# A shifted-window transformer block: unit 0's first norm ahead of the pipeline's steps, and 32x32 block transposes of neighbouring tokens

## The chip, the cores and the metric

The kernel runs on one core of one Trainium2 chip. The metric is the device time of one execution in microseconds. Five engines work from queues of their own, each in program order: TensorE (PE, with its weight loads as PEld), VectorE (DVE), ScalarE (ACT), GpSimd (POOL) and SyncE (SP), which here issues nearly all DMAs.

## The reference

`x` is [16, 192, 56, 56] in fp32 (batch, channels, height, width). Cut to what matters:

```python
xl = transpose(x, (0, 2, 3, 1))                       # channels last
xl = (xl - mean) * rsqrt(var + 1e-5) * n1w + n1b      # first norm, over the 192 channels
xl = roll(xl, (-3, -3), axis=(1, 2))                  # shifted windows of 7x7 tokens
q, k, v = split(xw @ qkv_w.T + qkv_b)                 # 6 heads of 32
attn = softmax(q @ k.T * 32 ** -0.5)                  # within each window, no mask
out = (attn @ v) @ proj_w.T + proj_b
xl = roll(windows back to the image, (3, 3))
xl = layernorm(xl, n2w, n2b)                          # second norm
h = gelu(xl @ fc1_w.T + fc1_b) @ fc2_w.T + fc2_b      # 192 -> 768 -> 192
return transpose(h, (0, 3, 1, 2)) + x
```

The first norm's mean and variance belong to a token (one pixel), over its 192 channels, while the input and all activations lie with channels in partitions.

## The kernel before, in words

**Units.** The work is cut into 128 units (`UNITS`): one row of eight 7x7 windows of one image, T = 392 tokens. A unit passes through a software pipeline. Each engine's program is written out by hand as a `step(t, k, it)` function in which `u[lag]` is the unit `t - lag`, or None where that is outside 0 to 127, and `steps` (L470) emits the steps t = 0 to 134. The order of the calls within a step is the order of the engine's queue. TensorE works on QKV of unit t, attention of t - 1, projection of t - 2 and the MLP of t - 3 (L621). VectorE's numbering begins earlier, with the transposes: QKV of unit u on TensorE needs what VectorE does in its step u + 2.

**First norm.** SP loads each unit twice. `load_groups` (L382) puts it into `xg`, of which partition 32r + c holds channel c of each group of 32 for the tokens 128r to 128r + 127; `load` (L374) puts it into `xt` with channels in partitions. `token_blocks` (L948) is one VectorE instruction that transposes `xg` in blocks of 32x32 into `xtok`, tokens in partitions; block b of the four (`PAIRS`) takes every fourth token, so partition p then holds tokens 4p to 4p + 3. `stats(0, u, j)` and `mean_var(0, u, j)` (L966, L975) reduce the channels to mean and variance in `mv[0]`, four tokens a partition. GpSimd's `rstd` (L1185) makes 1/sqrt(var + eps) with a power. `stats_out` (L391) stores `mv[0]` to a little DRAM tensor in the order of the tokens, 32 bytes a partition, in one DMA, and `stats_in` (L398) broadcasts it to all partitions (`bc`, 392 KB). Then `less_mean` and `times_rstd` (L955, L962; channels 0 to 127, VectorE) and `less_mean_rest` and `times_rstd_rest` (L1194, L1201; channels 128 to 191, GpSimd) normalise. ScalarE's `hi_part` (L718) rounds that to the high part `x1_h` (and `x_r`), and VectorE's `lo_part` (L1000) subtracts for the low part. TensorE's `values` and `qkv` wait for `lo_part("x1", u, 1)`.

**Weights.** All weights are split into high and low parts on VectorE: those of QKV in `first_weights` (L911), which `less_mean(0)` calls and which also waits for TensorE's products of the bias (L505); all others, with the biases, in `other_weights` (L928), which `lo_part("x1", 0, 1)` calls. `other_weights` begins with a wait for ten small loads (`s_rest`), which SP issues at L424 to L432, behind `stats_out(0)`, `stats_in(0)`, `load_groups(2)` and `load(0, 1)`. The projection on TensorE waits for its end.

**SP's queue.** After the start (L413 to L432) each step (L447) is: `load_groups(t)`; for t below 7 also `load`; `stats_in(t - 2)`; the second half of `spread(t - 4)` and the first of `spread(t - 3)`, which copy V into the block-diagonal tile `vbd` once VectorE's `v_out` (L1061) has evicted it from PSUM; `stats_out(t - 1)`; then `store` (L405), which waits for GpSimd's `residual`, and the `load` that it makes room for.

**GpSimd's queue** (L1222) takes in one step, among others, `rstd(0, u[0])`, `less_mean_rest(u[1])`, `times_rstd_rest(u[1])` and then `rstd(1, u[4])`, the second norm's, on which VectorE's `normalise` (L983) waits.

Of the kernel before, what the change touches and what calls it, by code (L numbers as in the profile page):

```python
# [24 lines left out]
ALU = mybir.AluOpType  # L25
# [9 lines left out]
T = NW * N  # L35
# [6 lines left out]
PAIRS = NW // 2  # L42
# [57 lines left out]
def swin_block_program(nc, x, n1w, n1b, qkv_wt, qkv_b, proj_wt, proj_b, n2w, n2b,  # L100
                       fc1_wt, fc1_b, fc2_wt, fc2_b, out):
    ctx = ExitStack()
    with ctx:
        def sb(name, shape, dt=F32):
            return ctx.enter_context(nc.sbuf_tensor(name, shape, dt))
# [29 lines left out]


        xt = sb("xt", [128, SLOTS, 2, T])
        st = [sb(f"st{i}", [TP, PAIRS, 6]) for i in range(2)]
        mv = [sb(f"mv{i}", [TP, PAIRS, 2]) for i in range(2)]
        ve = [sb(f"ve{i}", [TP, PAIRS]) for i in range(2)]  # L140
        rs = sb("rs", [TP, PAIRS])


# [229 lines left out]
        def _(sp):  # L373
# [17 lines left out]
            def stats_out(u):  # L391
                sp.wait_ge(s_rs[0], nth(u, 1, 0))
                if u > 1:

                    sp.wait_ge(s_mr[u % 2], 16 * (u // 2))
                sp.dma_start(spread_out[u % 2].rearrange("(p b) q -> p b q", b=PAIRS), mv[0][:, :, :]).then_inc(s_mr_out, 16)

            def stats_in(u):  # L398
                sp.wait_ge(s_mr_out, 16 * (u + 1))
                if u > 1:  # L400
                    sp.wait_ge(s_ym1, nth(u - 2, 1, 0))
                    sp.wait_ge(s_yr1, nth(u - 2, 1, 0))
                sp.dma_start(bc[:, u % 2], spread_out[u % 2:u % 2 + 1].to_broadcast([128, T, 2])).then_inc(s_mr[u % 2], 16)
# [66 lines left out]
        def steps(step):  # L470

            for t in range(UNITS + LAGS):
                step(t, t % SLOTS, t // SLOTS)
# [405 lines left out]
        def _(dve):  # L879
# [68 lines left out]
            def token_blocks(u):  # L948
                dve.wait_ge(s_xg[u % XG], 16 * sum(len(group_runs(v % UPB)) for v in range(u % XG, u + 1, XG)))
                if u == 0:  # L950
                    dve.wait_ge(s_xg_zero, 1)
                nc.vector.transpose(xtok.rearrange("p b (c d) -> p c b d", d=32),
                                    xg[:, u % XG].rearrange("p c (t b) -> p c b t", b=PAIRS)).then_inc(s_tr, 1)

            def less_mean(u, k):  # L955
                if u == 0:
                    assert first_weights() == 4
                dve.wait_ge(s_mr[u % 2], 16 * (u // 2 + 1))
                dve.wait_ge(s_x[k], (u // SLOTS + 1) * transfers(k))
                nc.vector.tensor_tensor(ym1[:, :], xt[:, k, 0, :], bc[:, u % 2, :, 0], ALU.subtract).then_inc(s_ym1_sub, 1)  # L960

            def times_rstd(u):  # L962
                dve.wait_ge(s_ym1_sub, nth(u, 1, 0))
                nc.vector.tensor_tensor(ym1[:, :], ym1[:, :], bc[:, u % 2, :, 1], ALU.mult).then_inc(s_ym1, 1)

            def stats(ln, u, j):  # L966
                if ln == 0:
                    dve.wait_ge(s_tr, nth(u, 1, 0))
                    nc.vector.bn_stats(st[0][:, j, :], xtok[0:TP, j, :]).then_inc(s_stats[0], 1)
                    return  # L970
                if j % 2 == 0:
                    dve.wait_ge(s_pe["ln2"], nth(u, 2, j // 2))
                nc.vector.bn_stats(st[1][:, j, :], ln_chunk("ln2", j)).then_inc(s_stats[1], 1)

            def mean_var(ln, u, j):  # L975
                if j == 0:
                    dve.wait_ge(s_stats[ln], nth(u, PAIRS, PAIRS - 1))
                    if ln == 0 and u > 0:

                        dve.wait_ge(s_mr_out, 16 * u)  # L980
                nc.vector.bn_aggr(mv[ln][:, j, :], st[ln][:, j, :]).then_inc(s_mv[ln], 1)  # L981

            def normalise(ln, u, j):  # L983
# [16 lines left out]
            def lo_part(name, u, g):  # L1000
                xh, xl, xrr = HI_LO[name]
                lo, m, hi = ((xl, CM, xh), (xrr[CR:128], CR, xrr[0:CR]))[g]
                if name == "o":
                    dve.wait_ge(s_hi[name], nth(u, 5, 0))
                elif name == "x2":
                    dve.wait_ge(s_hi[name], nth(u, 3, 0))
                else:
                    dve.wait_ge(s_hi[name], nth(u, 2, g))
                src = evicted(name, g, m)
                if name == "o":  # L1010

                    nc.vector.scalar_tensor_tensor(out=lo, in0=src, scalar=bq[0:m, g:g + 1], in1=hi.bitcast(F32),
                                                   op0=ALU.add, op1=ALU.subtract).then_inc(s_lo[name], 1)
                else:
                    nc.vector.tensor_tensor(lo, src, hi.bitcast(F32), ALU.subtract).then_inc(s_lo[name], 1)
                if name == "x1" and g == 1 and u == 0:
                    other_weights(4)

            def hidden_lo(u, m):

# [47 lines left out]
            def step(t, k, it):  # L1068
# [2 lines left out]
                    less_max(u[4], 2)  # L1071
                    row_sum(u[4], 0)
                if u[1] is not None:
                    mean_var(0, u[1], 0)
                if u[4] is not None:
                    row_max(u[4], 3)
                    row_sum(u[4], 1)
                    row_scale(u[4], 0)
                if u[1] is not None:
                    mean_var(0, u[1], 1)  # L1080
                if u[6] is not None:
                    x2_rest_lo(u[6])
                if u[1] is not None:
                    mean_var(0, u[1], 2)
                if u[4] is not None:
                    less_max(u[4], 3)
                if u[5] is not None:
# [1 line left out]
                if u[7] is not None:  # L1089
                    finish_main(u[7], (k - 7) % SLOTS)  # L1090
                if u[1] is not None:
                    mean_var(0, u[1], 3)
                if u[3] is not None:
                    v_out(u[3], 0)
                if u[5] is not None:
# [1 line left out]
                if u[3] is not None:  # L1097
                    v_out(u[3], 1)
                if u[0] is not None:
                    token_blocks(u[0])  # L1100
                if u[5] is not None:
                    stats(1, u[5], 0)
                if u[0] is not None:
                    stats(0, u[0], 0)
                if u[7] is not None:
                    finish_rest(u[7])
                if u[5] is not None:
# [3 lines left out]
                if u[5] is not None:  # L1111
                    stats(1, u[5], 2)
                if u[2] is not None:
                    less_mean(u[2], (k - 2) % SLOTS)
                if u[6] is not None:
                    hidden_lo(u[6], 0)
                if u[5] is not None:
# [9 lines left out]
                if u[5] is not None:  # L1127
                    mean_var(1, u[5], 3)
                if u[2] is not None:
                    times_rstd(u[2])  # L1130
                if u[6] is not None:
                    hidden_lo(u[6], 1)
                    hidden_lo(u[6], 2)
                if u[0] is not None:
                    stats(0, u[0], 1)
                if u[4] is not None:
                    row_sum(u[4], 3)
                if u[5] is not None:
                    normalise(1, u[5], 0)
                    normalise(1, u[5], 1)  # L1140
                if u[0] is not None:
                    stats(0, u[0], 2)
                if u[5] is not None:
                    normalise(1, u[5], 2)
                    normalise(1, u[5], 3)
                if u[4] is not None:
                    row_scale(u[4], 3)
                if u[2] is not None:
                    lo_part("x1", u[2], 0)
                if u[3] is not None:  # L1150
                    row_max(u[3], 0)
                if u[6] is not None:
# [8 lines left out]
                if u[6] is not None:  # L1161
                    hidden_lo(u[6], 4)
                if u[2] is not None:
                    lo_part("x1", u[2], 1)
                if u[3] is not None:
                    row_max(u[3], 2)
                if u[0] is not None:
                    stats(0, u[0], 3)

            steps(step)  # L1170


        @block.gpsimd
        def _(pool):
# [10 lines left out]
            def rstd(ln, u):  # L1185

                pool.wait_ge(s_mv[ln], nth(u, PAIRS, PAIRS - 1))
                nc.gpsimd.tensor_tensor(ve[ln][:, :], mv[ln][:, :, 1], eps[0:TP, :], ALU.add).then_inc(s_ve[ln], 1)  # L1188
                pool.wait_ge(s_ve[ln], nth(u, 1, 0) + (2 if ln == 0 else 0))

                to = rs[:, :] if ln else mv[0][:, :, 1]
                nc.gpsimd.tensor_tensor(to, ve[ln][:, :], half[0:TP, 0:PAIRS], ALU.pow).then_inc(s_rs[ln], 1)

            def less_mean_rest(u, k):  # L1194
                pool.wait_ge(s_mr[u % 2], 16 * (u // 2 + 1))
                pool.wait_ge(s_x[k], (u // SLOTS + 1) * transfers(k))
                if u > 0:
                    pool.wait_ge(s_lo["x1"], nth(u - 1, 2, 1))
                nc.gpsimd.tensor_tensor(yr1[:, :], xt[0:CR, k, 1, :], bc[0:CR, u % 2, :, 0], ALU.subtract).then_inc(s_yr1_sub, 1)
# [22 lines left out]
            def step(t, k, it):  # L1222
                u = units(t)
                if u[4] is not None:
                    scaled_probs(u[4], 3)
                if u[6] is not None:
                    hidden_lo_last(u[6])
                if u[3] is not None:
                    scaled_probs(u[3], 0)
                if u[0] is not None:  # L1230
                    rstd(0, u[0])
                if u[1] is not None:
                    less_mean_rest(u[1], (k - 1) % SLOTS)
                    times_rstd_rest(u[1])
                if u[4] is not None:
                    rstd(1, u[4])
                if u[3] is not None:
                    scaled_probs(u[3], 1)
                if u[6] is not None:
                    residual(u[6], (k - 6) % SLOTS)  # L1240
                if u[3] is not None:
                    scaled_probs(u[3], 2)

            steps(step)


# [23 lines left out]
```

## Time and profile before

| | us |
|---|---|
| median of 3 runs | 2939.3 (2938.61 to 2942.02) |
| profiled execution, its own time | 2939.99 |
| its span | 2938.2 |
| PE, PEld busy in the span | 2888.9 (98%), 2820.7 (96%) |
| DVE, ACT busy | 2692.8 (92%), 2689.2 (92%) |
| POOL busy | 1365.5 (46%) |
| DMA, mean share of the 16 engines, q1 | 30.9% |

The span runs from the first to the last instruction of the profiled execution; its own time is 1.8 us more. Matmuls are pipelined, so that a busy PE is not PE at its peak. The granted TensorE clock has a mean of 0.999 of full speed. In the lists of waits a wait is put down to what came last by semaphore.

### The profile page before, as it was taken

What the parts mean: (1) busy time and instruction counts of PE and PEld (TensorE: products, weight loads), DVE (VectorE), ACT (ScalarE), POOL (GpSimd) and SP (SyncE); (2) the same over time, 40 slices, a digit from 0 to 9 for tenths busy, and PEclk for the clock granted to TensorE, in tenths of its full rate; (3) what the DMA queues carried; (4) which work ended last, traced back from release to release, by engine and by line L of the source; (5) the groups of instructions that cost most, each with busy time, mean ns of one, the idle gap of its engine ahead of it and who ended that gap; (6) DMA issues with size and microseconds to landing.
All of it is one profiled execution on the core that took longest, in us unless ns stands there. A gap on an engine that the chain in (4) does not pass through costs nothing.

```text
span 2938.2 us, 75046 instructions
## 1 busy us (share of the span) xinstructions
PE 2888.9 (98%) x26284; PEld 2820.7 (96%) x26284; DVE 2692.8 (92%) x7211; ACT 2689.2 (92%) x5500; POOL 1365.5 (46%) x1549
## 2 busy tenths in 40 slices
PE   4999999999999999999999999999999999999998
PEld 4999999999999999999999999999999999999998
DVE  7899999999999999999999999999999999999985
ACT  3899999999999999999999999999999999999996
POOL 3444444444444444444544444444445444444442
PEclk9999999999999999999999999999999999999999
DMA  5233333333333332333233233333333333333321
GB/s 111 61 76 75 70 75 75 74 68 78 77 70 71 74 78 68 75 78 70 71 74 78 69 73 79 70 69 77 78 70 71 76 76 69 75 75 73 69 60 26
DMA packets 606164, 213.11 MB, mean 73 GB/s; under 512 B 461411, under 2 KB 589156, under 8 KB 605796
## 3 DMA queue, kind: packets, MB, share of 16 engines
q1 hardware_dynamic: 601860, 206.64, 30.9%
q8 instruction: 217, 3.56, 0.5%
q10 hardware_dynamic: 3936, 1.68, 0.3%
q14 instruction: 151, 1.24, 0.1%
HBM read 130.69 MB, written 38.94 MB: 58 GB/s over the span
## 4 chain that ended last, share of the span: by engine, by line
PE 97%; DVE 1%; ACT 1%; SPq 0%; DMA 0%; issue 0%; POOL 0%; POOLq 0%; ACTq 0%
PE psum L318 8%; PE psum L319 7%; PE psum L320 7%; PE psum L322 7%; PE psum L321 7%; PE psum L600 7%; PE psum L574 6%; PE psum L554 5%; PE psum L565 5%; PE psum L555 5%; PE psum L566 5%; PE psum L556 5%; PE psum L580 4%; PE psum L328 4%; PE psum L330 3%; PE psum L329 3%
## 5 line engine op out<-in xcount | busy, mean ns | idle before, releaser
L1215 POOL TENSOR_TENSOR pr<-pr,rc 98x294 f32<-98x294 f32 x512 | 385.9, 764 | 382.3 <-DVE rc L1059 382.3
L756 ACT ACTIVATE hh<-psum,b 128x392 fp32r<-128x392 f32 x768 | 451.7, 588 | 46.2 <-PE psum L566 37.5
L759 ACT ACTIVATE hf<-psum,b 128x392 f32<-128x392 f32 x768 | 451.7, 588 | 6.3
L1188 POOL TENSOR_TENSOR ve<-mv,eps 98x4 f32<-98x4 f32 x256 | 80.9, 316 | 768.1 <-DVE mv L981 768.1
L1209 POOL TENSOR_TENSOR hl<-hf,hh 128x392 fp32r<-128x392 f32 x128 | 226.0, 1766 | 374.3 <-ACT hf L759 374.3
L1046 DVE TENSOR_REDUCE mx<-psum 98x6 f32<-98x294 f32 x512 | 232.3, 454 | 133.0 <-PE psum L575 129.0
L1023 DVE TENSOR_TENSOR hl<-hf,hh 128x392 fp32r<-128x392 f32 x640 | 347.7, 559 | 3.8 <-ACT hf L759 3.7
L318 PE MATMUL psum<-x_h,w_mh 128*128 128x392 f32 x768 | 275.0, 358 | 0.7 <-DVE pr L1051 0.6
L554 PE MATMUL psum<-hh,w2h 128*128 128x392 f32 x768 | 272.8, 355 | 0.0
L713 ACT ACTIVATE pt<-psum 113x294 f32<-113x294 f32 x512 | 207.1, 405 | 70.4 <-PE psum L580 70.2
L574 PE MATMUL psum<-km,qm 128*98 128x98 f32 x2048 | 261.0, 249 | 7.4 <-ACT qm L716 4.0
L565 PE MATMUL psum<-hl,w2h 128*128 128x392 f32 x768 | 264.5, 344 | 0.3 <-POOL hl L1209 0.3
L555 PE MATMUL psum<-hh,w2l 128*128 128x392 f32 x768 | 261.8, 341 | 0.0
L319 PE MATMUL psum<-x_h,w_ml 128*128 128x392 f32 x768 | 261.4, 340 | 0.0
L320 PE MATMUL psum<-x_l,w_mh 128*128 128x392 f32 x768 | 260.9, 340 | 0.0
L566 PE MATMUL psum<-hl,w2h 128*64 128x392 f32 x768 | 260.4, 339 | 0.0
L322 PE MATMUL psum<-x_r,w_rl 128*128 128x392 f32 x768 | 260.4, 339 | 0.0
L321 PE MATMUL psum<-x_r,w_rh 128*128 128x392 f32 x768 | 260.3, 339 | 0.0
L556 PE MATMUL psum<-hh,w2r 128*128 128x392 f32 x768 | 259.4, 338 | 0.0
L574 PEld LDWEIGHTS psum<-km,qm 128*98 128x98 f32 x2048 | 237.0, 166 | 11.3 <-ACT qm L716 4.6
L1051 DVE TENSOR_TENSOR pr<-psum,mx 98x294 f32<-98x294 f32 x512 | 234.2, 457 | 4.2
L768 ACT ACTIVATE pr<-pr 98x294 f32<-98x294 f32 x512 | 230.2, 450 | 7.7 <-DVE pr L1051 3.1
(144 smaller groups left out, 10410.3 us busy)
## 6 DMA issues: line engine op xcount, KB each, us to landing
bc<-mean_rstd SPq DMA_DIRECT2D x128, 392.0 KB, 3.7
vbd<-vs SPq DMA_DIRECT2D x1024, 36.8 KB
xg<-in_x SPq DMA_DIRECT2D x368, 96.0 KB, 2.4
xt<-in_x SPq DMA_DIRECT2D x112, 194.5 KB, 2.7
out<-xt SPq DMA_DIRECT2D x112, 194.5 KB, 1.9
xt<-in_x SPq DMA_DIRECT2D x112, 97.2 KB, 2.4
out<-xt SPq DMA_DIRECT2D x112, 97.2 KB, 2.1
xg<-in_x SPq DMA_DIRECT2D x128, 3.8 KB, 2.0
```

The costliest lines, as they stand in the source:

```text
L318: nc.tensor.matmul(ps, wmh[:, c0:c0 + m], xh, start=True, stop=False)
L319: nc.tensor.matmul(ps, wml[:, c0:c0 + m], xh, start=False, stop=False)
L320: nc.tensor.matmul(ps, wmh[:, c0:c0 + m], xl, start=False, stop=False)
L321: nc.tensor.matmul(ps, wrh[:, c0:c0 + m], xrr, start=False, stop=False)
L322: return nc.tensor.matmul(ps, wrl[:, c0:c0 + m], xrr, start=False, stop=True)
L554: nc.tensor.matmul(ym, w2h[:, m, 0:CM], hh[:, b, :], start=a, stop=False)
L555: nc.tensor.matmul(ym, w2l[:, m, :], hh[:, b, :], start=False, stop=False)
L565: nc.tensor.matmul(ym, w2h[:, m, 0:CM], hl[:, b, :], start=False, stop=z)
L566: nc.tensor.matmul(yx[0:CR], w2h[:, m, CM:C], hl[:, b, :], start=False, stop=z, skip_group_check=True).then_inc(s_pe["fc2"], 1)
L574: nc.tensor.matmul(ps[:, TP * wi:TP * wi + TP], qm[:, w, :], km[:, w, :], start=True, stop=True)
L756: nc.scalar.activation(hh[:, m % HB, :], bank("fc1", m)[:, 0:T], ACT.Gelu, bias=b1[:, m:m + 1]).then_inc(s_hh, 1)
L759: nc.scalar.activation(hf[:, m % HB, :], bank("fc1", m)[:, 0:T], ACT.Gelu, bias=b1[:, m:m + 1]).then_inc(s_gelu, 1)
```

## The change

It has three parts. (1) Unit 0's whole first norm (`token_blocks`, `stats`, `mean_var`, `less_mean` with `first_weights`, `times_rstd`, `lo_part`) stands on VectorE ahead of `steps`; behind it come unit 1's transpose, statistics and `mean_var`, then `other_weights(4)`. On GpSimd `rstd(0, 0)` and the two operations for channels 128 to 191 of unit 0 stand ahead of its steps. The calls for these units are left out of the steps by conditions; the other engines' order is not touched. Unit 2's statistics, which step 2 had around `less_mean(0)`, stay in step 2, now behind `other_weights`. (2) Block b of a transpose takes 32 neighbouring tokens: the source is contiguous where it had a stride of four floats, and partition 32r + t holds tokens 128r + 32b + t for b = 0 to 3. The 104 partitions that then hold tokens (`LP[0]`) take the place of 98. (3) `stats_out` becomes four DMAs with pieces of 8 bytes, 128 in each of three and 8 in the last, and the waits on `s_mr_out` count four times as much.

```diff
+        LP = (96 + T % 128, TP)
+        st = [sb(f"st{i}", [LP[i], PAIRS, 6]) for i in range(2)]
...
-                sp.dma_start(spread_out[u % 2].rearrange("(p b) q -> p b q", b=PAIRS), mv[0][:, :, :]).then_inc(s_mr_out, 16)
+                for r in range(3):
+                    sp.dma_start(spread_out[u % 2, 128 * r:128 * r + 128].rearrange("(b t) q -> t b q", b=PAIRS), mv[0][32 * r:32 * r + 32]).then_inc(s_mr_out, 16)
+                sp.dma_start(spread_out[u % 2, 384:T], mv[0][96:LP[0], 0, :]).then_inc(s_mr_out, 16)
...
             def stats_in(u):
-                sp.wait_ge(s_mr_out, 16 * (u + 1))
+                sp.wait_ge(s_mr_out, 16 * 4 * (u + 1))
...
                 nc.vector.transpose(xtok.rearrange("p b (c d) -> p c b d", d=32),
-                                    xg[:, u % XG].rearrange("p c (t b) -> p c b t", b=PAIRS)).then_inc(s_tr, 1)
+                                    xg[:, u % XG].rearrange("p c (b t) -> p c b t", b=PAIRS)).then_inc(s_tr, 1)
...
-                    nc.vector.bn_stats(st[0][:, j, :], xtok[0:TP, j, :]).then_inc(s_stats[0], 1)
+                    nc.vector.bn_stats(st[0][:, j, :], xtok[0:LP[0], j, :]).then_inc(s_stats[0], 1)
...
-                        dve.wait_ge(s_mr_out, 16 * u)
+                        dve.wait_ge(s_mr_out, 16 * 4 * u)
...
-                if name == "x1" and g == 1 and u == 0:
-                    other_weights(4)
...
                 if u[1] is not None:
-                    mean_var(0, u[1], 0)
+                    if u[1] > 1:
+                        mean_var(0, u[1], 0)
...
                 if u[0] is not None:
-                    token_blocks(u[0])
+                    if u[0] > 1:
+                        token_blocks(u[0])
...
                 if u[2] is not None:
-                    less_mean(u[2], (k - 2) % SLOTS)
+                    if u[2] > 0:
+                        less_mean(u[2], (k - 2) % SLOTS)
...
+            token_blocks(0)
+            for j in range(PAIRS):
+                stats(0, 0, j)
+            for j in range(PAIRS):
+                mean_var(0, 0, j)
+            less_mean(0, 0)
+            times_rstd(0)
+            lo_part("x1", 0, 0)
+            lo_part("x1", 0, 1)
+
+            token_blocks(1)
+            for j in range(PAIRS):
+                stats(0, 1, j)
+            for j in range(PAIRS):
+                mean_var(0, 1, j)
+            other_weights(4)
             steps(step)
...
                 if u[0] is not None:
-                    rstd(0, u[0])
-                if u[1] is not None:
-                    less_mean_rest(u[1], (k - 1) % SLOTS)
-                    times_rstd_rest(u[1])
+                    if u[0] > 0:
+                        rstd(0, u[0])
+                if u[1] is not None:
+                    if u[1] > 0:
+                        less_mean_rest(u[1], (k - 1) % SLOTS)
+                    if u[1] > 0:
+                        times_rstd_rest(u[1])
...
+            rstd(0, 0)
+            less_mean_rest(0, 0)
+            times_rstd_rest(0)
             steps(step)
```

The remaining calls of `stats(0, ...)`, `mean_var(0, ...)`, `times_rstd` and `lo_part("x1", ...)` in VectorE's step get the same conditions (`u[0] > 1`, `u[1] > 1`, `u[2] > 0`).

## Rows read from the trace of the kernel before

**Rows 1.** Windows of all engines: busy us (instructions), TensorE's clock, DMA share, GB/s

```profile
0.00:100.00 100.00, 58.98 (x466) 56.14 (x467) 78.19 (x210) 43.63 (x93) 33.90 (x50) 0.98 0.48 104
100.00:2880.00 2780.00, 2780.00 (x25425) 2718.89 (x25424) 2582.76 (x6922) 2609.44 (x5334) 1314.93 (x1483) 1.00 0.32 72
```

**Rows 2.** Who waited for whom, TensorE, 95 to 2938 us: total, times, longest

```profile
PE psum L318 <- DVE pr L1051: 0.6, 1, 0.6
```

**Rows 3.** The same, TensorE, 0 to 95 us

```profile
PE psum L328 <- DVE x_r L1015: 17.5, 2, 16.3
...
PE psum L574 <- DVE xn L986: 3.4, 1, 3.4
```

**Rows 4.** The chain of waits, 12 to 36 us: start, us, what

```profile
12.74 2.21 DMA mean_rstd<-mv
...
17.31 8.56 DMA xg<-in_x
```

**Rows 5.** Timeline, VectorE, TensorE, ScalarE: start, us, engine, line, what [idle before]

```profile
8.48 1.14 DVE L969 BATCH_NORM_STATS2 st<-xtok 98x6 f32<-98x192 f32 x4
...
9.66 0.38 DVE L981 BATCH_NORM_AGGREGATE mv<-st 98x2 f32<-98x6 f32 x4
...
18.25 0.58 PE L506 MATMUL psum<-nwb,raw_q_r 64*128 64x1 f32 x2
...
21.96 1.28 ACT L713 ACT_TABLE_LOAD   x1 [21.96 <-issue]
...
33.26 0.56 ACT L713 ACTIVATE x_h<-ym 128x392 fp32r<-128x392 f32 x1 [10.01 <-DVE ym L964]
...
35.05 0.28 DVE L930 CAST pb_hi<-pb 1x256 fp32r<-1x256 f32 x1
...
35.16 0.45 PE L328 MATMUL psum<-wq_mh,x_h 128*98 128x192 f32 x1 [16.33 <-DVE x_r L1015]
...
43.98 0.35 DVE L969 BATCH_NORM_STATS2 st<-xtok 98x6 f32<-98x192 f32 x1
...
44.94 0.56 DVE L1066 COPY vs<-psum 98x384 f32<-98x384 f32 x1 [0.20 <-PE psum L332]
...
47.08 1.58 DVE L952 STREAM_TRANSPOSE xtok<-xg 128x768 f32<-128x768 f32 x1
```

**Rows 6.** Timeline, SP's issues, 0 to 100 us

```profile
28.69 0.47 SPq L432 DMA_DIRECT2D b<-in_fc_b  x1
...
45.53 3.49 SPq L444 DMA_DIRECT2D vbd<-vs  x4
...
55.08 6.69 SPq L444 DMA_DIRECT2D vbd<-vs  x8
...
67.05 1.40 SPq L403 DMA_DIRECT2D bc<-mean_rstd  x1
...
80.43 0.52 SPq L403 DMA_DIRECT2D bc<-mean_rstd  x1
```

**Rows 7.** DMA issues: direction, engine, count, KB each, median us to landing

```profile
bc<-mean_rstd SPq DMA_DIRECT2D x128, 392.0 KB, 3.7
...
xt<-in_x SPq DMA_DIRECT2D x128, 1.5 KB, 2.2
```

**Rows 8.** Instruction groups by shape, VectorE: count | busy us, mean ns | idle before

```profile
L952 DVE STREAM_TRANSPOSE xtok<-xg 128x768 f32<-128x768 f32 x128 | 202.0, 1578 | 12.8 <-DMA xg<-in_x 12.7
...
L943 DVE TENSOR_TENSOR w2l<-raw,w2h 128x768 fp32r<-128x768 f32 x1 | 1.0, 959 | 0.0
```

**Rows 9.** SP's own waits, 100 to 2880 us

```profile
SPq L408 <- POOL xt L1220: 741.7, 124, 6.9
```

**Rows 10.** Timeline, GpSimd, 60 to 100 us

```profile
71.83 1.04 POOL L1199 TENSOR_TENSOR yr<-xt,bc 64x392 f32<-64x392 f32 x1 [0.76 <-DMA bc<-mean_rstd]
...
75.83 0.43 POOL L1188 TENSOR_TENSOR ve<-mv,eps 98x4 f32<-98x4 f32 x1 [1.84 <-DVE mv L981]
...
90.11 1.04 POOL L1199 TENSOR_TENSOR yr<-xt,bc 64x392 f32<-64x392 f32 x1
```

More of the change, by code:

```diff
@@ L137, in swin_block_program @@
         xt = sb("xt", [128, SLOTS, 2, T])
-        st = [sb(f"st{i}", [TP, PAIRS, 6]) for i in range(2)]
-        mv = [sb(f"mv{i}", [TP, PAIRS, 2]) for i in range(2)]
-        ve = [sb(f"ve{i}", [TP, PAIRS]) for i in range(2)]
+        LP = (96 + T % 128, TP)
+        st = [sb(f"st{i}", [LP[i], PAIRS, 6]) for i in range(2)]
+        mv = [sb(f"mv{i}", [LP[i], PAIRS, 2]) for i in range(2)]
+        ve = [sb(f"ve{i}", [LP[i], PAIRS]) for i in range(2)]
         rs = sb("rs", [TP, PAIRS])
@@ L1079, in step @@
                 if u[1] is not None:
-                    mean_var(0, u[1], 1)
+                    if u[1] > 1:
+                        mean_var(0, u[1], 1)
                 if u[6] is not None:
@@ L1083, in step @@
                 if u[1] is not None:
-                    mean_var(0, u[1], 2)
+                    if u[1] > 1:
+                        mean_var(0, u[1], 2)
                 if u[4] is not None:
@@ L1091, in step @@
                 if u[1] is not None:
-                    mean_var(0, u[1], 3)
+                    if u[1] > 1:
+                        mean_var(0, u[1], 3)
                 if u[3] is not None:
@@ L1103, in step @@
                 if u[0] is not None:
-                    stats(0, u[0], 0)
+                    if u[0] > 1:
+                        stats(0, u[0], 0)
                 if u[7] is not None:
@@ L1129, in step @@
                 if u[2] is not None:
-                    times_rstd(u[2])
+                    if u[2] > 0:
+                        times_rstd(u[2])
                 if u[6] is not None:
@@ L1134, in step @@
                 if u[0] is not None:
-                    stats(0, u[0], 1)
+                    if u[0] > 1:
+                        stats(0, u[0], 1)
                 if u[4] is not None:
@@ L1141, in step @@
                 if u[0] is not None:
-                    stats(0, u[0], 2)
+                    if u[0] > 1:
+                        stats(0, u[0], 2)
                 if u[5] is not None:
@@ L1148, in step @@
                 if u[2] is not None:
-                    lo_part("x1", u[2], 0)
+                    if u[2] > 0:
+                        lo_part("x1", u[2], 0)
                 if u[3] is not None:
@@ L1163, in step @@
                 if u[2] is not None:
-                    lo_part("x1", u[2], 1)
+                    if u[2] > 0:
+                        lo_part("x1", u[2], 1)
                 if u[3] is not None:
@@ L1167, in step @@
                 if u[0] is not None:
-                    stats(0, u[0], 3)
+                    if u[0] > 1:
+                        stats(0, u[0], 3)
+            token_blocks(0)
[13 more added lines that the diff above has]
+            other_weights(4)
             steps(step)
@@ L1187, in rstd @@
                 pool.wait_ge(s_mv[ln], nth(u, PAIRS, PAIRS - 1))
-                nc.gpsimd.tensor_tensor(ve[ln][:, :], mv[ln][:, :, 1], eps[0:TP, :], ALU.add).then_inc(s_ve[ln], 1)
+                nc.gpsimd.tensor_tensor(ve[ln][:, :], mv[ln][:, :, 1], eps[0:LP[ln], :], ALU.add).then_inc(s_ve[ln], 1)
                 pool.wait_ge(s_ve[ln], nth(u, 1, 0) + (2 if ln == 0 else 0))
                 to = rs[:, :] if ln else mv[0][:, :, 1]
-                nc.gpsimd.tensor_tensor(to, ve[ln][:, :], half[0:TP, 0:PAIRS], ALU.pow).then_inc(s_rs[ln], 1)
+                nc.gpsimd.tensor_tensor(to, ve[ln][:, :], half[0:LP[ln], 0:PAIRS], ALU.pow).then_inc(s_rs[ln], 1)
             def less_mean_rest(u, k):
```

## The prediction

> **What bounds the kernel now.** I read the busy table by windows first. From 100 to 2880 us TensorE is busy in all of 2780 us, and of the first 100 us it works in 59.0 [rows 1]. So the body is bound by TensorE, with VectorE at 93% and ScalarE at 94% of that stretch, and only the 41 idle us in front can be won. The waits confirm it: after 95 us TensorE waits for others three times, the longest 0.6 us [rows 2]. Before 95 us its large wait for another engine's arithmetic is 16.3 us, for the low part of unit 0's `x_r`; a later one of 3.4 us is put down to the second norm's `xn` [rows 3]. The chain of waits says why the first came so late: unit 0's statistics were landed at 14.95, but the chain goes on through the load of unit 2's groups (8.56 us) [rows 4]. VectorE runs in order, and in the old order unit 2's transpose, which waits for that load until 25.89, stood ahead of `first_weights` and `less_mean(0)`. The first QKV matmul is at 35.16 [rows 5].
>
> **Part 1, unit 0's norm first.** After the change VectorE goes from `mean_var(0,0,3)` (done by 10.1, [rows 5]) straight to the first weights. The bias products on TensorE must end (about 18.8, [rows 5]), then unit 0's broadcast must land. SP now issues four transfers in place of one: three more at about 0.5 us, the last at 14.25 and landed 2.2 us after its issue [rows 4], so `stats_in(0)` goes out at 16.5, 1.5 later, and lands by 21 to 22. ScalarE is free only after its own weight issues and a table load, 21.96 + 1.28 = 23.24 [rows 5]. It made `x_h` at 33.26; it will at about 23.25. Everything up to the first matmul moves by 10.0 us, to 25.2.
>
> **Part 2, what that meets next.** Ten microseconds would be 0.34%, but VectorE's next long piece, `other_weights`, begins with a wait for all small loads (`s_rest`), and these stand on SP behind `stats_out(0)` and `stats_in(0)`. Their last issue was at 28.69 [rows 6]; now 30.2. A small load takes 2.2 us to land [rows 7], so the piece begins at 32.4. It took from 35.05 to 43.98, 8.9 us [rows 5], so it ends at 41.4: a lead of 2.6, not 10. Before, VectorE had unit 2's transpose and three of its four statistics behind it by then; now all of them come after, with the aggregates. By rows that is 1.14 + 0.38 [rows 5] and a transpose, some 2.5 in all: 43.9. Two evictions of V of 0.56 follow [rows 5] without a wait, since TensorE has done unit 0's V by then. Unit 3's transpose starts at 45.0 in place of 47.08 [rows 5]: lead 2.1.
>
> **Part 3, the transpose.** It cost 1.58 us with a source stride of four floats; after the change the source is contiguous. No row has a contiguous transpose. Bounds: 1.58 (nothing changes), and 0.96, a subtraction over the same 128x768 floats [rows 8]. I take 1.0, because the old time is two thirds above the engine's other work on that count and the stride is what sets its operand apart. The Trainium skill, SBUF — State Buffer, section "Door 1: The DMA port swizzle", says that each access that crosses to a new 16-byte line pays a penalty; the old pattern crosses with every float, so by that rule the transpose gets faster, and no row here separates stride from transposing. In the body the 0.6 us a unit is worth nothing, since TensorE sets the pace there; if the transpose stays at 1.58, the front loses 0.6 us of its lead.
>
> **Part 4, SP's queue.** Per unit three more issues cost 1.45 us. In the body they are hidden: SP waits for GpSimd at the store right behind `stats_out`, 742 us in 124 waits, 6.0 us each [rows 9], and `stats_in` reads them a whole step later. The DMA rings carry some 300 more packets of 8 bytes a unit at a 32% share [rows 1]: nothing. In the front SP is not free. There it runs without a pause from unit 0's spread (issued from 45.53 on, when V's eviction ends) to `stats_in(3)` at 67.05 [rows 6]. Unit 0's first eviction of V now ends about 1.1 earlier (44.4), and two `stats_out` (units 2 and 3) lie between: `stats_in(3)` at 67.05 - 1.1 + 2.9 = 68.9. Its broadcast had landed by 71.83 [rows 10], 4.8 after the issue, and takes 3.7 at the median [rows 7]; take 4.2: landed at 73.1. GpSimd's two operations take 2.2 (it already waited 0.76 us for this very load [rows 10]), to 75.3, and behind them in its queue stands `rstd(1,0)`, which started at 75.83 on VectorE's aggregates [rows 10] and, through `xn`, ended TensorE's 3.4 us wait. With the lead of VectorE it would be ready near 73; it now waits for GpSimd until about 75.1 to 75.3. **The lead left is 0.6 to 0.7 us.** `stats_in(4)` moves from 80.43 [rows 6] to 83.7, lands at 87.4, and GpSimd wants it only at 90.11 [rows 10]: nothing more is lost, and SP catches up in the wait inside the next spread.
>
> By the Trainium skill, DMA: Bandwidth & Descriptors, section "Specifications", transfers under 512 bytes lead to a read-modify-write and miss the line rate; the stores were 32 bytes a partition and are 8 bytes now, so the rule speaks against the change. It gives no time for this case, and the old stores, already under its limit, landed in 2.2 us.
>
> **The sum.** -10.0 at the first matmul, of which 7.4 are lost at `s_rest`, 0.5 more to unit 2's statistics, 0.6 returned by a transpose, and all but 0.7 eaten by SP's longer queue: -0.7. The profiled execution took 2940.0 us for a span of 2938.2, 0.7 above the median of 2939.3. Against it the sum gives 2939.3, on the median 2938.6. A measurement of this kernel (runs 2938.6 to 2942.0) tells about 0.2% (5.9 us) from no change.
>
> **Rivals.** (a) *The ten microseconds survive.* That needs `s_rest` landed before VectorE asks and SP never late: 2929.3. For it: the first matmul surely comes early, and the 16.3 us wait is the largest there is. Against it: with SP not shifted at all, 28.69 + 2.2 = 30.9 allows `other_weights` a lead of 4.2 at most, and the broadcasts still follow SP's queue. 4%.
> (b) *SP becomes the bound of the front, and the end comes later.* With y us more per `stats_out`, `s_rest` moves by y and `stats_in(3)` by 3y - 2.5, so `xn` begins at 72.4 + 3y against 77.4: even at y = 1.7, slower from there. If an issue of 128 small pieces costs what a spread's issue does (eight in 6.69, 0.84 each [rows 6]), y = 2.5 and the time is 2939.3 + 2.5 = 2941.8; the longest issue in the rows, 1.40, gives y = 4.2 and +7.6, 2946.9, over the 0.2%. For it: SP has no gap there. Against: other issues of 98 and more rows cost 0.45 to 0.6. 20% for a slower end at all, 4% beyond 0.2%.
> (c) *The new order does not reach the first matmul*, because the broadcast of unit 0 now shares the rings with the MLP's weights (unit 2's groups took 8.56 us there). At 8.6 it lands at 25.1, and the first matmul is 7 instead of 10 earlier. The second step hides that, since `s_rest` sets it: still 2938.6. 10%, in the same range.
>
> **How the numbers follow.** The forecast, a gain of 0 to 3 us, 68%; (b) 20%, (c) hides in the forecast's range; (a) 4%; the rest, 8%, is the transpose at 1.58 with slower landings, 0 to +1. Bounds: the lead of 4.2 us that an unshifted SP would allow, with 0.3 us of the runs' scatter, gives 2934.8; y = 2.5 with another microsecond of landing gives 2942.8. So the range is 2934.8 to 2942.8. Faster by over 0.2%: 0.05, slower 0.04, within it 0.91.
>
> **What would show it.** Right: the first QKV matmul near 25; a VectorE gap of about 4 us ahead of `other_weights`; four `stats_out` issues of 0.45 to 0.6; GpSimd waiting for `bc` of units 2 and 3; `rstd(1,0)` near 75; and a body in which TensorE never waits. Wrong: `other_weights` starting near 28, `rstd(1,0)` before 72 or after 79, or the step from 100 to 2880 us changed by more than 1 us.

## The result, and the profile after

The changed kernel takes 2945.5 us (22 runs, 2943.9 to 2947.2) beside 2940.7 for the kernel before (22 runs): ratio 1.0015, 95% interval 1.0009 to 1.0021. It is 4.8 us slower, where 0.7 us faster was forecast. The page of its profiled execution:

```profile
span 2942.2 us, 75430 instructions
...
PE 2891.6 (98%) x26284; PEld 2823.3 (96%) x26284; DVE 2631.7 (89%) x7211; ACT 2686.1 (91%) x5500; POOL 1365.2 (46%) x1549
...
q1 hardware_dynamic: 644868, 206.66, 32.3%
```

The windows (columns as in [rows 1], with the tail as a third row):

```profile
0.00:100.00 100.00, 57.58 (x440) 54.43 (x441) 72.95 (x193) 39.26 (x84) 32.66 (x46) 0.93 0.50 96
100.00:2880.00 2780.00, 2780.00 (x25428) 2719.25 (x25427) 2524.27 (x6932) 2607.14 (x5336) 1312.01 (x1482) 1.00 0.33 73
2880.00:2942.20 62.20, 54.01 (x420) 49.62 (x418) 34.52 (x88) 39.73 (x82) 20.57 (x22) 0.98 0.11 28
```

TensorE's body is what it was: busy in all of 2780 us. Its tail and its front are not comparable at fixed marks, since everything lies later: it works 57.6 us in the first 100, 1.4 less than in [rows 1], though its first QKV matmul comes five microseconds sooner. VectorE's body fell from 2583 to 2524 us, and the one group of instructions that fell with it is the transpose:

```profile
L956 DVE STREAM_TRANSPOSE xtok<-xg 128x768 f32<-128x768 f32 x128 | 123.9, 968 | 0.1
```

968 ns in place of 1578 [rows 8], 78 us over all units, while the engine's whole busy time fell by 61. Who waited for whom, TensorE, first before 95 us, then after it:

```profile
PE psum L330 <- DVE x_r L1019: 15.4, 2, 11.0
...
PE psum L584 <- POOL pr L1246: 3.5, 1, 3.5
PE psum L578 <- DVE xn L990: 3.5, 1, 3.5
PE psum L578 <- DVE vs L1068: 3.1, 1, 3.1
```

```profile
PE psum L320 <- DVE pr L1053: 0.6, 1, 0.6
```

The body has the one wait of 0.6 us that it had [rows 2]. In the front the wait for `x_r` went from 16.3 to 11.0 us [rows 3], the one for `xn` (L578) stayed, and two are new: 3.5 us for GpSimd's scaled probabilities and 3.1 us for VectorE's evictions of V (the latter comes with the new order: the order alone has it too, with 3.0). SP's issues (compare [rows 6]; L399 and L400 are the four stores, L390 the group loads, L407 the broadcasts):

```profile
12.73 1.58 SPq L399 DMA_DIRECT2D mean_rstd<-mv  x3
14.36 0.38 SPq L400 DMA_DIRECT2D mean_rstd<-mv  x1
18.59 0.35 SPq L407 DMA_DIRECT2D bc<-mean_rstd  x1
...
31.93 0.47 SPq L436 DMA_DIRECT2D b<-in_fc_b  x1
...
36.69 5.11 SPq L390 DMA_DIRECT2D xg<-in_x  x5
...
46.09 3.50 SPq L448 DMA_DIRECT2D vbd<-vs  x4
...
51.12 1.31 SPq L400 DMA_DIRECT2D mean_rstd<-mv  x1
52.86 4.49 SPq L390 DMA_DIRECT2D xg<-in_x  x5
...
59.73 0.50 SPq L407 DMA_DIRECT2D bc<-mean_rstd  x1
...
73.51 0.52 SPq L407 DMA_DIRECT2D bc<-mean_rstd  x1
```

Four readings. The last store of unit 0 was issued at 14.36 and the broadcast behind it not until 18.59. The last small load went at 31.93, 3.2 later than before. Behind the stores of units 1 and 2 the five group loads took 5.11 and 4.49 us. So the broadcasts of units 2 and 3 went out at 59.73 and 73.51, where the latter had gone at 67.05. VectorE and TensorE in the same stretch:

```profile
26.04 0.57 DVE L964 TENSOR_TENSOR ym<-xt,bc 128x392 f32<-128x392 f32 x1 [6.00 <-DMA bc<-mean_rstd]
...
34.14 0.28 DVE L934 CAST pb_hi<-pb 1x256 fp32r<-1x256 f32 x1 [1.57 <-DMA b<-in_fc_b]
...
43.07 0.97 DVE L956 STREAM_TRANSPOSE xtok<-xg 128x768 f32<-128x768 f32 x1
...
45.54 0.99 DVE L1068 COPY vs<-psum 98x384 f32<-98x384 f32 x2
...
63.56 0.57 DVE L964 TENSOR_TENSOR ym<-xt,bc 128x392 f32<-128x392 f32 x1 [2.26 <-DMA bc<-mean_rstd]
```

```profile
30.12 0.45 PE L330 MATMUL psum<-wq_mh,x_h 128*98 128x192 f32 x1 [11.02 <-DVE x_r L1019]
...
67.00 1.39 PE L584 MATMUL psum<-ident,pr 98*128 98x98 f32 x6 [3.51 <-POOL pr L1246]
```

`other_weights` (L934, its first instruction) waits for the small loads and starts at 34.14, 0.9 earlier than before; unit 2's transpose is at 43.07, the evictions of V at 45.54, and unit 3's transpose follows at 46.5, 0.6 earlier than in [rows 5]; and unit 2's `less_mean` waits 2.26 us for its broadcast. GpSimd:

```profile
63.60 1.40 POOL L1230 TENSOR_TENSOR yr<-xt,bc 64x392 f32<-64x392 f32 x1 [4.82 <-DMA bc<-mean_rstd]
...
66.27 2.28 POOL L1246 TENSOR_TENSOR pr<-pr,rc 98x294 f32<-98x294 f32 x3
...
78.75 1.03 POOL L1230 TENSOR_TENSOR yr<-xt,bc 64x392 f32<-64x392 f32 x1 [2.21 <-DMA bc<-mean_rstd]
...
82.15 0.43 POOL L1219 TENSOR_TENSOR ve<-mv,eps 98x4 f32<-98x4 f32 x1 [1.26 <-DVE mv L985]
```

It stood idle for 4.82 us until unit 2's broadcast had landed, and only then came to the probabilities (L1246) that TensorE waited for; `rstd(1, 0)` started at 82.15, in place of 75.83 [rows 10]. The trace's chain of waits leads from that broadcast through GpSimd's probabilities, TensorE's attention and projection and VectorE's aggregates to this `rstd`. The same chain, which in [rows 4] went through unit 2's groups, now names the store, the last small load and the broadcast of unit 2:

```profile
14.36 4.21 DMA mean_rstd<-mv
...
31.93 2.19 DMA b<-in_fc_b
...
59.73 3.81 DMA bc<-mean_rstd
```

### The profile page after: what moved, and what is told of

Same layout as the page of the kernel before. It is cut to its first block, busy times and chain, and to the rows that moved or that the text cites. A ratio compares the mean times of both kernels' runs of the same rounds, so it can differ in the third digit from the quotient of the medians.

```text
span 2942.2 us, 75430 instructions
## 1 busy us (share of the span) xinstructions
PE 2891.6 (98%) x26284; PEld 2823.3 (96%) x26284; DVE 2631.7 (89%) x7211; ACT 2686.1 (91%) x5500; POOL 1365.2 (46%) x1549
## 3 DMA queue, kind: packets, MB, share of 16 engines
q14 instruction: 154, 1.26, 0.3%
## 4 chain that ended last, share of the span: by engine, by line
PE 97%; SPq 1%; DVE 1%; DMA 0%; ACT 0%; issue 0%; POOL 0%; POOLq 0%; DVEq 0%; ACTq 0%
PE psum L320 7%; PE psum L321 7%; PE psum L322 7%; PE psum L324 7%; PE psum L323 7%; PE psum L604 7%; PE psum L578 6%; PE psum L558 5%; PE psum L569 5%; PE psum L559 5%; PE psum L570 5%; PE psum L560 5%; PE psum L584 4%; PE psum L330 4%; PE psum L332 3%; PE psum L331 3%
## 5 line engine op out<-in xcount | busy, mean ns | idle before, releaser
L1246 POOL TENSOR_TENSOR pr<-pr,rc 98x294 f32<-98x294 f32 x512 | 385.4, 762 | 377.7 <-DVE rc L1061 377.7
L1219 POOL TENSOR_TENSOR ve<-mv,eps 104x4 f32<-104x4 f32 (+1 forms) x256 | 80.6, 315 | 746.9 <-DVE mv L985 746.9
L578 PE MATMUL psum<-km,qm 128*98 128x98 f32 x2048 | 261.4, 250 | 8.1 <-DVE xn L990 3.5
L977 DVE BATCH_NORM_STATS2 st<-psum 98x6 f32<-98x192 f32 x512 | 184.1, 360 | 73.3 <-PE psum L334 68.6
L578 PEld LDWEIGHTS psum<-km,qm 128*98 128x98 f32 x2048 | 237.5, 166 | 11.9 <-issue 7.1
```

Source lines behind the costliest of these rows:

```text
L578: nc.tensor.matmul(ps[:, TP * wi:TP * wi + TP], qm[:, w, :], km[:, w, :], start=True, stop=True)
```

## The experiments

Each was timed in five rounds beside the kernel before on the same chip. In the code, `...` marks what is left out. Five theories were at stake. S: the small stores hold up SP's queue in the front. O: the new order itself costs. I or P: of the stores, the number of issues or the size of the pieces sets the price. F: the first matmul, later than forecast, is what made it slow.

**The order alone and the layout alone.** The first is the changed kernel with the old layout, the second the old order with the new transpose and stores. For the first the lines below are changed (and the waits' counts and `LP` with them); the second keeps the new ones and has the old order:

```diff
-                for r in range(3):
-                    sp.dma_start(spread_out[...].rearrange("(b t) q -> t b q", b=PAIRS), mv[0][32 * r:32 * r + 32])...
-                sp.dma_start(spread_out[u % 2, 384:T], mv[0][96:LP[0], 0, :])...
+                sp.dma_start(spread_out[u % 2].rearrange("(p b) q -> p b q", b=PAIRS), mv[0][:, :, :])...
-                                    xg[:, u % XG].rearrange("p c (b t) -> p c b t", b=PAIRS))...
+                                    xg[:, u % XG].rearrange("p c (t b) -> p c b t", b=PAIRS))...
```

> Unit 0's first norm in front, but the old transpose and the old single store of 32 bytes a partition. Theory S (the four small stores hold up SP's queue in the front): the first matmul near 25 us, the last small load issued near 29 and other_weights from about 31, a lead of 2 to 4 us kept to the end, so 2936.5 to 2939 beside 2940.7 of the kernel before (ratio 0.9985 to 0.9995). Rival O (the order itself costs, since unit 2's statistics now stand behind other_weights): no faster than before, ratio 1.000 to 1.001.

> The old order with the new transpose and the four stores of 8-byte pieces. Theory S: the transpose falls from 1.58 to 0.97 us without effect on the body, stats_in(0) goes out near 18.6 instead of 15.0, and the front ends 4 to 7 us later: ratio 1.0013 to 1.0024, as slow as the changed kernel or slower. Rival O: within 1 us of the kernel before.

Measured: the order alone 2939.9 us beside 2941.6, ratio 0.9994 (0.9985 to 1.0003); the layout alone 2949.0, ratio 1.0023 (1.0013 to 1.0033). By medians -1.7 and +7.4 us, in sum 5.7 where both together made 4.8. The interval of the first touches 1, so a gain from the order alone is likely and not certain; that the layout is what costs is shown. With the order alone `other_weights` began where the small loads let it; the last of them was issued at 28.43 and took 3.79 us to land:

```profile
32.24 0.28 DVE L932 CAST pb_hi<-pb 1x256 fp32r<-1x256 f32 x1 [4.31 <-DMA b<-in_fc_b]
```

**Which part of the stores.** The kernel before with its one store cut in four, by partitions (pieces of 32 bytes) and by the token in the partition (pieces of 8 bytes):

```diff
+                for r in range(4):
+                    n = min(128, T - 128 * r)
+                    sp.dma_start(spread_out[u % 2, 128 * r:128 * r + n].rearrange("(p b) q -> p b q", b=PAIRS), mv[0][32 * r:32 * r + n // PAIRS])...
```

```diff
+                for b in range(4):
+                    sp.dma_start(spread_out[u % 2].rearrange("(p b) q -> p b q", b=PAIRS)[:, b], mv[0][:, b, :])...
```

> The kernel before with its store cut into four by partitions (32, 32, 32 and 2), pieces still of 32 bytes. If the number of issues sets the price (theory I): 1.4 us more of SP's queue a unit, stats_in(0) 1.5 later, and the end 1.5 to 3 us later (ratio 1.0005 to 1.001). If the size of the pieces does (theory P): SP's queue longer by the same 1.4, but loads behind the stores are issued as fast as before, and the landing stays at 2.2 us.

> The kernel before with its store cut into four by the token in the partition: four issues of 98 pieces of 8 bytes. Theory P: the last store lands 4 us after its issue, the group loads behind stats_out(2) and (3) stretch from 2.3 to 4.5 us or more, and the end is 3 to 6 us later (ratio 1.001 to 1.002), clearly more than four stores of 32-byte pieces. Theory I: the same as those.

Measured: 2943.4, ratio 1.0004 (0.9995 to 1.0013), and 2947.5, ratio 1.0020 (1.0011 to 1.0029). With the same number of issues the pieces of 8 bytes cost 4.2 us more. (The bytes are the same too, so there are four times as many pieces; their size and their number aren't separated.) SP's issues behind the stores, first by partitions (the group loads of units 3 and 4; those of unit 2 took 2.75), then by tokens (unit 0's broadcast, then the group loads of units 2, 3 and 4):

```profile
34.39 2.26 SPq L388 DMA_DIRECT2D xg<-in_x  x5
...
51.38 2.29 SPq L388 DMA_DIRECT2D xg<-in_x  x5
```

```profile
16.40 0.35 SPq L404 DMA_DIRECT2D bc<-mean_rstd  x1
16.79 3.99 SPq L388 DMA_DIRECT2D xg<-in_x  x5
...
35.27 4.07 SPq L388 DMA_DIRECT2D xg<-in_x  x5
...
54.38 4.06 SPq L388 DMA_DIRECT2D xg<-in_x  x5
```

2.75, 2.26 and 2.29 us against 3.99, 4.07 and 4.06. So the stretched group loads come with the pieces (theory P). What is left for the number of issues (theory I) is 1.8 us by medians, which isn't clear of noise. One part of P's expectation missed: these last stores of 8 bytes (rows 32 bytes apart) let the broadcast go at 16.40, about 2 us behind the last store's issue, and not 4.

**One store with the new transpose.** The order alone, with the transpose of neighbouring tokens put back in:

```diff
-                                    xg[:, u % XG].rearrange("p c (t b) -> p c b t", b=PAIRS))...
+                                    xg[:, u % XG].rearrange("p c (b t) -> p c b t", b=PAIRS))...
```

> The new order with the new transpose of 32 neighbouring tokens, but one store of 32 bytes from 98 partitions: the statistics then go to other tokens' places, and six partitions' are not stored, so this leaves part of the norm out. Theory S (the stores alone make the change slow): the transpose 0.97 us, no effect on the body, the front 0 to 1.2 us earlier than with the old transpose, 2938.5 to 2940 beside 2941.5 of before (ratio 0.9990 to 0.9996), some 6 us under the changed kernel. Rival T (the transpose or the 104 partitions cost something): no better than the changed kernel's 1.0015.

Measured: 2937.6 beside 2941.0, ratio 0.9990 (0.9981 to 0.9998), below the range of the expectation's times. This kernel leaves part of the norm out, as said, and takes its statistics on 98 partitions; an instruction of them takes 349 ns at the median on 104 partitions (the changed kernel) and on 98 (the kernel before). The transpose costs nothing; by medians it gained one or two microseconds in the front. With the changed kernel's order and transpose, the one store in place of four is worth 8.2 us (-3.4 against +4.8): this is the plainest measure of what the four stores cost.

**The small loads first.** On SP, `load_groups(2)` and `load(0, 1)` behind the weights of the projection and the small loads, in the order-alone kernel, in the changed kernel and in the kernel before:

```diff
             stats_in(0)
-            load_groups(2)
-            load(0, 1)
...
             sp.dma_start(b2[0:CR, 1:2], fc2_b[CM:C]...
+            load_groups(2)
+            load(0, 1)
```

> The new order with the old transpose and store, and on SP the projection's weights and the ten small loads moved ahead of load_groups(2) and load(0, 1). Theory S: s_rest lands near 26 instead of 30.9, other_weights starts about 28.5 and not 32, the spread of unit 0 and with it SP's whole front come 2 to 3 us earlier than with the order alone: 2936 to 2938 beside 2941.5 (ratio 0.9980 to 0.9990). Rival B (other_weights was no limit in the front): the same as the order alone, 0.9994.

> The changed kernel with the same move on SP. Theory S: other_weights starts near 31 (after unit 1's statistics, which follow a first matmul at 30) instead of 34.1, but the group loads behind the stores and the broadcasts still follow SP's queue: 2 to 3 us better than the changed kernel, ratio 1.0005 to 1.001. Rival B: 1.0015 as before.

> The kernel before with the small loads and the projection's weights ahead of load_groups(2) and load(0, 1) on SP. Theory S: unit 2's transpose, which stands ahead of first_weights, waits for its groups longer, so the first matmul comes 3 to 8 us later and other_weights with it: slower than before by 3 to 8 us, ratio 1.001 to 1.0027. The move is worth something with the new order only. Rival B' (SP's small loads are a limit in either order): faster than before.

Measured: 2935.5 beside 2941.0, ratio 0.9983 (0.9974 to 0.9991); 2943.5, ratio 1.0010 (1.0001 to 1.0019); and 2944.4 beside 2940.4, ratio 1.0015 (1.0006 to 1.0023). The first is the fastest kernel of the study and beats both. Its last small load was issued at 23.93, 4.5 sooner than in the order alone, but took 5.94 us to land in place of 3.79, so `other_weights` gained 2.4:

```profile
29.89 0.28 DVE L933 CAST pb_hi<-pb 1x256 fp32r<-1x256 f32 x1 [2.06 <-DMA b<-in_fc_b]
```

In the old order the same move costs 4 us: the first matmul waits for unit 2's groups, and comes at 38.6. So the order of SP's loads is a limit only once VectorE's order no longer waits for the groups.

**Unit 0's broadcast sooner.** The changed kernel with `load_groups(1)` behind `stats_in(0)`:

```diff
-            load_groups(1)
             stats_out(0)
             stats_in(0)
+            load_groups(1)
```

> The changed kernel with load_groups(1) moved behind stats_in(0) on SP, so that unit 0's four stores go out at 11 and its broadcast near 15 or 16, at the time at which ScalarE issues the MLP's weights (15.4). Theory W (in the changed kernel unit 0's broadcast waits behind those weights): it lands by 20 to 22 instead of 26.0 and the first matmul comes near 25 instead of 30. Theory S says that this alone is worth little at the end, since other_weights and SP's queue decide: 0 to 2 us under the changed kernel, ratio 1.0008 to 1.0015. Rival F (the late first matmul is what made the change slow): 4 to 5 us gained, ratio 1.000 or lower.

Measured: 2946.1 beside 2940.4, ratio 1.0019 (1.0010 to 1.0028). The first QKV matmul and the first instruction of `other_weights`:

```profile
26.21 0.45 PE L330 MATMUL psum<-wq_mh,x_h 128*98 128x192 f32 x1 [5.87 <-DVE x_r L1019]
```

```profile
35.00 0.28 DVE L934 CAST pb_hi<-pb 1x256 fp32r<-1x256 f32 x1 [4.75 <-DMA b<-in_fc_b]
```

The matmul came 3.9 us earlier than in the changed kernel, and nothing came of it: `other_weights` began 0.9 later, as the small loads did. The expectation had 0 to 2 us less than the changed kernel; it came out 0.9 above. Theory F falls: a first matmul 3.9 us earlier was worth nothing. The broadcast landed by 22.2; it had gone out at 16.65, some 4 us behind the last store again, so the slow landing of the stores is not due to the group loads ahead of them.

**The loads behind the broadcasts.** The fastest kernel with SP's loads of units 2 to 6 behind `stats_in`:

```diff
-                    if 1 < t < AHEAD:
-                        load(0, t)
                 if 0 <= t - 2 < UNITS:
                     if t - 2 > 0:
                         stats_in(t - 2)
+                if 1 < t < AHEAD:
+                    load(0, t)
```

> The best version so far (new order, old transpose and store, small loads first) with the loads of units 2 to 6 moved behind stats_in in SP's steps. Theory S: the broadcasts of units 1 to 4 go out 2.2 us sooner, GpSimd's waits for bc of units 2 and 3 (1.06 and 0.64 us) go, and the end comes 0.5 to 2 us earlier: 2934 to 2935, ratio 0.9978 to 0.9982. If SP no longer limits the front: 0.9983 as without the move.

Measured: 2935.7 beside 2940.4, ratio 0.9984 (0.9975 to 0.9993). No gain over the version without the move: GpSimd's waits for the broadcasts of units 2 and 3 are gone, as expected, and by the expectation's own mark SP no longer limited the front. `rstd(1, 0)` still waited 2.66 us, for VectorE's aggregates.

The marks of the front in all runs, each from its own profiled execution (us):

| kernel | first QKV matmul | `other_weights` | `rstd(1, 0)` | median less that of before |
|---|---|---|---|---|
| before | 35.2 | 35.1 | 75.8 | 0 |
| changed | 30.1 | 34.1 | 82.2 | +4.8 |
| order alone | 24.9 | 32.2 | 76.0 | -1.7 |
| layout alone | 37.3 | 37.2 | 84.0 | +7.4 |
| order and near transpose, one store | 25.2 | 31.8 | 74.6 | -3.4 |
| four stores, 32 bytes | 35.3 | 35.2 | 77.9 | +1.8 |
| four stores, 8 bytes | 38.2 | 38.1 | 82.3 | +6.0 |
| order, small loads first | 24.8 | 29.9 | 72.7 | -5.4 |
| changed, small loads first | 29.8 | 32.2 | 80.6 | +2.6 |
| before, small loads first | 38.6 | 38.5 | 78.9 | +4.0 |
| changed, broadcast sooner | 26.2 | 35.0 | 82.5 | +5.7 |
| order, small loads first, loads behind | 25.0 | 29.0 | 72.3 | -4.7 |

The end follows `rstd(1, 0)` within 2.3 us, and hardly the first matmul.

## Why the prediction was wrong

**Part 1, the first matmul: direction right, size off.** Forecast 25.2, measured 30.1. The term that failed is the landing of the stores: 2.2 us after the last issue, taken from a store of 32-byte pieces; it was 4.2. And what I had as rival (c) came on top: the broadcast, issued behind ScalarE's loads of the MLP's weights (15.4 to 17.8), took 7.4 us. From its landing to the matmul there were 4.1 us, where rival (c) had 3.1: VectorE's `times_rstd` took 1.27 us in place of 0.57, and `x_r` was made only then. The DMA engines from 17 to 23 us of the changed kernel:

```profile
q10 hardware_dynamic: 716, 1.08, 80.2%
...
raw<-in_fc_wt ACTq DMA_DIRECT2D x1, 576.0 KB, 9.2
bc<-mean_rstd SPq DMA_DIRECT2D x1, 392.0 KB, 7.4
```

Only ScalarE's queue (q10) moved packets in that stretch; SP's (q1) has none, though the broadcast had been issued at 18.59. Over all runs, unit 0's broadcast took 4.4 to 5.5 us where it was issued between 14.9 and 16.7 (eight kernels) and 7.2 to 7.4 between 18.3 and 18.8 (three), but in one it took 7.7, issued at 16.40 behind the four stores by tokens. That the weights held it up is therefore likely and not shown. In the order-alone kernel, whose broadcast went at 15.0, the matmul came at 24.9, as forecast.

**Part 2, `s_rest`: right.** `other_weights` waited for the small loads and not for VectorE's own work: forecast 32.4, measured 34.1, and the 1.7 between are the store's landing again, since the small loads stand behind `stats_in(0)`. That the ten microseconds would be lost there is shown by the order alone (first matmul 10.3 earlier, `other_weights` 2.8) and by the version with the small loads first, which ended 3.7 us earlier still. One term was luck: 2.2 us for a small load to land held in the changed kernel (2.19), but in the order alone it was 3.79, and with the small loads first 5.94.

**Part 3, the transpose: right.** 1.0 was taken and 0.97 measured. The rule of the Trainium skill, SBUF — State Buffer, "Door 1: The DMA port swizzle", that crossing to a new 16-byte line with each access pays a penalty, agrees with the trace, and the order alone and its version with the near transpose differ in the stride alone (1.58 against 0.97 us). No run tried another stride, so that it is the 16 bytes isn't shown. It was worth nothing in the body, as said.

**Part 4, SP's queue: the step that failed.** The kind of cause was right: SP late, a broadcast late, GpSimd late, `xn` late. Its size was not, and it came by another broadcast; `rstd(1, 0)` after 79 was one of the prediction's own signs of being wrong. The forecast put `stats_in(3)` at 68.9; it was issued at 73.5, 4.6 later. Three terms were too small. Unit 0's spread began at 46.1 and not at 44.4: 1.7, the landing of unit 0's stores again, by way of the small loads and `other_weights`. The stores of units 2 and 3 cost 2.3 and 1.3 more than the old one, and not 1.45 each: 0.7. And the group loads behind the stores of unit 2 took 4.5 us in place of 2.3: 2.2, for which the sum had no term at all. (Those behind unit 1's, 5.1, ended ahead of the wait for V at 46.1 and cost nothing.) SP's short pauses, 0.4 us more behind unit 2's stores and 0.4 less ahead of its broadcast, cancel; the latter pause, of half a microsecond from 54.2 in the kernel before, the prediction had overlooked. The broadcast then landed 5.2 us after its issue and not 4.2, so GpSimd was done with unit 3 at 80.9, where 75.3 was forecast. By the forecast's own path alone `rstd(1, 0)` would have come 5.1 us later than before.

The same terms, without unit 3's stores, had moved unit 2's broadcast, issued at 54.69 before, to 59.73, and this one, which the forecast did not follow, ended last, by 1.3 us. That is read from the chain of waits; no run moved this broadcast alone in the changed kernel. Its issue in the kernel before:

```profile
54.69 0.34 SPq L403 DMA_DIRECT2D bc<-mean_rstd  x1
```

GpSimd takes `less_mean_rest` ahead of unit 0's scaled probabilities, so TensorE waited for attention too, and `rstd(1, 0)` at 82.15 waited for VectorE's aggregates (1.26 us, in GpSimd's timeline above), no longer for GpSimd's work on unit 3. By rival (b)'s formula the measured start of `xn`, 83.7, would be y = 3.8. That rival's likely price was 2.5, from dearer issues of the stores. That isn't where it came from: with the new stores the issues took 1.3 to 1.5 us more at units 0, 1 and 3, about as forecast, and 2.3 only at unit 2; the rest came in the loads behind them and in the landing. So rival (b) had the right side and queue, at 20%, and only in part the right term.

The rule of the Trainium skill, DMA: Bandwidth & Descriptors, "Specifications", that transfers under 512 bytes lead to a read-modify-write and miss the line rate, was set aside because the old stores were under the limit too. The runs show neither a read-modify-write nor the limit, but they do show that far under it the cut of a store still matters: pieces of 8 bytes against 32 cost 4.2 us at an equal number of issues and bytes.

**The body: right.** SP's wait at the store absorbed the longer queue:

```profile
SPq L412 <- POOL xt L1251: 552.8, 123, 7.1
```

4.5 us on average in place of 6.0 [rows 9].

What stays open: why issues of group loads behind stores of 8 bytes take up to twice their time in the first three steps and not later (and not always there: behind unit 1's stores they took 2.26 us with the layout alone); and why the changed kernel's stores (neighbouring rows 8 bytes apart) land 4 us after the issue and those by tokens (32 bytes apart) in 2. No run separated those. The traces narrow it down. The changed kernel's queue on SP moved its last packet of unit 0's stores before 15.6 us, and the store that was waited for counted as landed only at 18.57. Behind the stores of units 1 and 2 it moved 3 packets from 38 to 39 us and 12 from 53 to 54, where four stores of 32-byte pieces left it 234 from 35 to 36; and of unit 2's five group loads it was a single issue, of 2.67 us, that took the time. So in these places the queue nearly stood still for three to four microseconds behind the small pieces, after their packets had gone; what it waited for isn't shown.

## What to carry to other kernels

In a pipelined kernel that one engine bounds, a change in the start is worth what reaches the last stage's first use, not what it does to the first matmul: write down, for each queue that fills the pipeline, the issues that a moved or split transfer pushes back, and follow them until some engine waits by itself. Splitting a store into pieces of 8 bytes for the sake of a faster vector instruction gave the time back, and more, in the queue that issues the transfers. When an engine is freed early, look at once for the semaphore it meets next, and move the loads behind that one forward together with it: alone the order gained 1.7 us by medians, which isn't clear of noise, with the loads 5.4, which is.

## What the runs showed of the hardware that was not expected

A broadcast of 392 KB issued 1 to 3 us after 1.3 MB of weights on another engine's queue moved no packet up to 23 us, 4.4 us after its issue, while that queue's did: 7.4 us to land, against 3.8 at the median. Part 1 above has the other runs, one of which doesn't fit.

The wait of TensorE in the front had a second price, its clock. The windows of the changed kernel (the first number behind the five engines is the granted clock) around its wait from 63 to 67 us:

```profile
64.00:66.00 2.00, 0.00 (x0) 0.00 (x0) 2.00 (x7) 0.54 (x1) 1.92 (x2) 0.96 0.25 39
66.00:68.00 2.00, 1.00 (x5) 0.81 (x6) 2.00 (x5) 0.23 (x2) 2.00 (x4) 0.50 0.34 53
...
70.00:72.00 2.00, 2.00 (x16) 1.83 (x16) 1.94 (x5) 0.76 (x2) 0.00 (x0) 0.50 0.27 6
...
74.00:76.00 2.00, 2.00 (x20) 1.98 (x19) 0.85 (x3) 1.97 (x6) 0.81 (x3) 1.00 1.11 222
```

It fell to 0.50, that is 1.2 of its 2.4 GHz, after the idle stretch and was back by 74. The six transposes at 67.00 took 1.39 us (TensorE's timeline above). The order alone has a like drop, 0.68 from 62 to 64 us and 0.50 from 64 to 66, so it isn't the stores' alone. In the kernel before no such drop lies there; it has one from 78 to 82, behind its own wait for `xn`, which the changed kernel does not have in that place. The same six in the kernel before, at the full clock:

```profile
62.84 0.67 PE L580 MATMUL psum<-ident,pr 98*128 98x98 f32 x6
```
